# Head statistics aggregated on GpSimd instead of VectorE in a three-stage decoder kernel

## The reference

```
def _ln(x, w, b):
    mu = mean(x, axis=-1);  var = mean(square(x - mu), axis=-1)
    return (x - mu) * rsqrt(var + EPS) * w + b

q  = _ln(fp8_linear(ln_out, wq,  wq_s,  q_in_scale ).reshape(b, s, 8, 2, 128), qln_w,  qln_b)
k  = _ln(fp8_linear(ln_out, wk,  wk_s,  k_in_scale ).reshape(b, s, 8, 128),    kln_w,  kln_b)
qx = _ln(fp8_linear(ln_out, wqx, wqx_s, qx_in_scale).reshape(b, s, 8, 2, 128), qxln_w, qxln_b)
kx = _ln((cond @ w_kv_x.T)[k half], kxln_w, kxln_b)
core = softmax(q k^T / sqrt(128)) v;   xout = softmax(qx kx^T / sqrt(128)) vx
out  = fp8_linear(concat(core, xout), wproj)
```

## Time and profile before

| | |
|---|---|
| median of three runs | 1904.36 us (1903.78 to 1906.09) |
| profiled execution, its own time | 1905.79 us |
| its span | 1902.8 us |
| mean granted TensorE clock | 0.978 |
| TensorE busy (product, weight load) | 1789.1 us (94%), 1251.0 us (66%) |
| VectorE busy | 1506.1 us (79%), 4917 instructions |
| ScalarE busy | 1065.9 us (56%) |
| GpSimd busy | 269.1 us (14%), 417 instructions |

### The profile page before, as it was taken

How to read it: one execution, slowest core, us unless ns; L and a number is a source line. 1 busy time by engine, 2 the same in 40 slices (tenths; PEclk the granted TensorE clock), 3 DMA queues, 4 the chain that set the end, 5 groups by cost and what they waited for, 6 DMA issues and landing times.

```text
span 1902.8 us, 32280 instructions
## 1 busy us (share of the span) xinstructions
PE 1789.1 (94%) x11024; PEld 1251.0 (66%) x11024; DVE 1506.1 (79%) x4917; ACT 1065.9 (56%) x2478; POOL 269.1 (14%) x417
## 2 busy tenths in 40 slices
PE   7999999548999999999999999999999999879998
PEld 3444444236877778877777777887877777644554
DVE  0165747387888888898889888888878888888997
ACT  1121211115666766766766766677656666667776
POOL 0000000011111111112111111212111112101111
PEclk9999999868999999999999999999999999989999
DMA  6000000202110200101110111011010102210000
GB/s 222 22 1 23 1 1 1 75 4 67 36 36 15 64 25 25 58 23 35 34 47 25 45 36 36 12 58 34 14 30 17 47 16 76 69 65 12 23 25 32
DMA packets 40448, 70.77 MB, mean 37 GB/s; under 512 B 2912, under 2 KB 21856, under 8 KB 39264
## 3 DMA queue, kind: packets, MB, share of 16 engines
q1 hardware_dynamic: 40288, 68.73, 10.9%
HBM read 63.47 MB, written 4.19 MB: 36 GB/s over the span
## 4 chain that ended last, share of the span: by engine, by line
PE 71%; DVE 15%; issue 8%; POOL 2%; ACT 2%; DMA 1%; POOLq 0%; SPq 0%; DVEq 0%; ACTq 0%
PE bank L368 18%; PE bank L424 14%; PE bank L478 10%; PE bank L534 8%; PE bank L573 5%; PE bank L498 4%; PE bank L609 3%; PE bank L484 3%; PE bank L457 2%; PE bank L451 1%; DVE nq L1084 1%; DVE nmx L1190 1%; ACT yb L823 1%; PE bank L542 1%; POOL rsC L1369 1%
## 5 line engine op out<-in xcount | busy, mean ns | idle before, releaser
L835 ACT ACTIVATE pr<-bank,nmx 128x512 f32<-128x512 f32 x256 | 174.9, 692 | 144.5 <-DVE nmx L1190 144.2
L424 PE MATMUL bank<-wqs,XQ 128*128 128x256 f16 x2048 | 249.5, 276 | 4.4 <-DVE x L1114 4.4
L478 PE MATMUL bank<-prT,KV 128*128 128x256 f32 x1024 | 244.5, 382 | 0.1
L534 PE MATMUL bank<-kT,qT 128*128 128x512 f32 x512 | 242.5, 596 | 0.7 <-ACT kT L768 0.7
L424 PEld LDWEIGHTS bank<-wqs,XQ 128*128 128x128 bf16 x2048 | 199.6, 100 | 45.4 <-issue 15.7
L478 PEld LDWEIGHTS bank<-prT,KV 128*128 128x128 f32 x1024 | 191.2, 192 | 52.1 <-issue 22.8
L1335 POOL TENSOR_TENSOR rdev<-gvar,cst 128x7 f32<-128x7 f32 x128 | 193.2, 1509 | 10.0
L823 ACT ACTIVATE yb<-bank,rsT 128x128 bf16<-128x128 f32 x512 | 146.7, 373 | 62.2 <-PE bank L484 62.2
L1333 POOL TENSOR_TENSOR gvar<-mvB,geps 128x7 f32<-128x7 f32 x128 | 29.0, 227 | 1052.6 <-DVE mvB L1074 1045.2
L1190 DVE TENSOR_REDUCE nmx<-bank 128x1 f32<-128x512 f32 x256 | 166.4, 679 | 8.8 <-PE bank L534 5.7
L573 PE MATMUL bank<-identf,pr 128*128 128x128 f32 x1024 | 153.0, 278 | 19.3 <-DVE pr L1094 18.8
(11 more groups left out here) (162 smaller groups left out, 3245.8 us busy)
## 6 DMA issues: line engine op xcount, KB each, us to landing
wst<-in_wcat SPq DMA_DIRECT2D x24, 512.0 KB, 4.0
wpst<-in_wproj SPq DMA_DIRECT2D x8, 1024.0 KB, 5.2
wa<-in_wgu SPq DMA_DIRECT2D x16, 512.0 KB, 3.6
xT<-in_xT SPq DMA_DIRECT2D x4, 1024.0 KB, 5.2
x<-in_x SPq DMA_DIRECT2D x4, 1024.0 KB, 12.1
wkx<-in_wkvx SPq DMA_DIRECT2D x8, 512.0 KB, 5.0
wa<-in_wdn SPq DMA_DIRECT2D x8, 512.0 KB, 3.6
wst<-in_wgu SPq DMA_DIRECT2D x4, 1024.0 KB, 5.2
```

Of the source, the lines that this page charges most:

```text
L424: ins = mm(dst, XQ[:, b, c, k, j * P:(j + 1) * P], w, start=(k == 0 and m == 0), stop=(k == KT - 1 and m == 1))
L478: mm(OB[:, 0:2 * P], KV[:, n % 2, t, P:2 * P], prT[:, st % 2, t, :, :].rearrange("p h s -> p (h s)"), start=(t == 0), stop=(t == ST - 1))
L534: mm(SB_[h][:], qT[:, h, st * P:(st + 1) * P], kT[:, :], start=True, stop=True).then_inc(s["scores_made"], 1)
L835: act_f(pr[:, h, :], SB_[h][:], ACT.Exp, bias=nmx[:, st, h:h + 1], accum_out=su[:, st, h:h + 1]).then_inc(s["exp_done"], 1)
```

## The change

`head_stats` on VectorE keeps the bn_stats and loses the wait and the aggregations; the memset now gives the signal to GpSimd. `deviations` on GpSimd works from what bn_stats leaves for each slot, the means of two halves (columns 1 and 4) and their sums of squared differences (columns 2 and 5): the difference of the means squared times 32, plus the two sums, plus 128 times the epsilon, is 128 times the variance with its epsilon. The power -0.5 of that is the former `rdev` times 128^-0.5. The factor is made good in the tables: queries are scaled by the weight alone (`hln`), with the offset times 128^-0.5 in `hlq`; keys by the weight times 128^0.5 (`hlk`). The mean is half the sum of the half means (`mnB`).

```diff
-        hlq = sb(ctx, "hlq", [P, 4])
+        hlq = sb(ctx, "hlq", [P, 2])
+        hlk = sb(ctx, "hlk", [P, 2])
...
-        mvB = sb(ctx, "mvB", [P, 7, 2])
+        mnB = sb(ctx, "mnB", [P, 7])
+        smB = sb(ctx, "smB", [P, 4, 7])
...
-                                ACT.Identity, scale=hlq[:, 2 * c:2 * c + 1], bias=hlq[:, 2 * c + 1:2 * c + 2])
+                                ACT.Identity, scale=hln[:, 4 * c:4 * c + 1], bias=hlq[:, c:c + 1])
...
-                act_f(kT[:, :], MB[:, :], ACT.Identity, scale=hln[:, 2:3], bias=hln[:, 3:4]).then_inc(s["kt_out"], 1)
+                act_f(kT[:, :], MB[:, :], ACT.Identity, scale=hlk[:, 0:1], bias=hln[:, 3:4]).then_inc(s["kt_out"], 1)
...
-            own.do(v.tensor_scalar(hlq[:, 0:2], hln[:, 0:2], float(P) ** -0.5, None, ALU.mult))
-            own.do(v.tensor_scalar(hlq[:, 2:4], hln[:, 4:6], float(P) ** -0.5, None, ALU.mult))
+            for i in range(2):
+                own.do(v.tensor_scalar(hlq[:, i:i + 1], hln[:, 4 * i + 1:4 * i + 2], float(P) ** -0.5, None, ALU.mult))
+                own.do(v.tensor_scalar(hlk[:, i:i + 1], hln[:, 4 * i + 2:4 * i + 3], float(P) ** 0.5, None, ALU.mult))
...
-            v.tensor_scalar(geps[:], gain[:], EPS, None, ALU.mult).then_inc(s["hlq_ready"], 1)
+            v.tensor_scalar(geps[:], gain[:], EPS * P, None, ALU.mult).then_inc(s["hlq_ready"], 1)
...
-                own.do(v.memset(pad[:], 0.0))
-                own.sync()
-                for h in slots:
-                    ins = v.bn_aggr(mvB[:, h, :], bnB[:, h, :])
-                ins.then_inc(s["bn_ready"], 1)
+                v.memset(pad[:], 0.0).then_inc(s["bn_ready"], 1)
...
-            own.do(v.memset(mvB[:], 0.0))
+            own.do(v.memset(bnB[:], 0.0))
...
                 pool.wait_ge(s["bn_ready"], tile + 1)
-                own.do(g.tensor_tensor(gvar[:], mvB[:, :, 1], geps[:], ALU.add))
+                own.do(g.tensor_tensor(smB[:, 0, :], bnB[:, :, 1], bnB[:, :, 4], ALU.subtract))
+                own.do(g.tensor_tensor(smB[:, 1, :], bnB[:, :, 2], bnB[:, :, 5], ALU.add))
+                own.do(g.tensor_tensor(smB[:, 2, :], bnB[:, :, 1], bnB[:, :, 4], ALU.add))
+                own.sync()
+                own.do(g.tensor_tensor(smB[:, 0, :], smB[:, 0, :], smB[:, 0, :], ALU.mult))
+                own.do(g.tensor_tensor(smB[:, 1, :], smB[:, 1, :], geps[:], ALU.add))
+                own.do(g.tensor_tensor(mnB[:], smB[:, 2, :], cst[:, 3, 0:7], ALU.mult))
+                own.sync()
+                own.do(g.tensor_tensor(smB[:, 3, :], smB[:, 0, :], cst[:, 0, 0:7], ALU.mult))
+                own.sync()
+                own.do(g.tensor_tensor(gvar[:], smB[:, 3, :], smB[:, 1, :], ALU.add))
                 own.sync()
                 g.tensor_tensor(rdev[:], gvar[:], CPOW, ALU.pow).then_inc(s["stats_ready"], 1)
```

More of the change, by code:

```diff
@@ L767, in kt_out @@
                 act.wait_ge(s["kt_made"], n + 1)
-                act_f(kT[:, :], MB[:, :], ACT.Identity, scale=hln[:, 2:3], bias=hln[:, 3:4]).then_inc(s["kt_out"], 1)
+                act_f(kT[:, :], MB[:, :], ACT.Identity, scale=hlk[:, 0:1], bias=hln[:, 3:4]).then_inc(s["kt_out"], 1)
             def kxt_out(u):
                 act.wait_ge(s["kxt_made"], u + 1)
-                act_f(kxT[:, :], P1[:, 256:256 + P], ACT.Identity, scale=hln[:, 6:7], bias=hln[:, 7:8]).then_inc(s["kxt_out"], 1)
+                act_f(kxT[:, :], P1[:, 256:256 + P], ACT.Identity, scale=hlk[:, 1:2], bias=hln[:, 7:8]).then_inc(s["kxt_out"], 1)
             act.wait_ge(s["yA_made"], ST * NB)
@@ L1060, in head_stats @@
                     v.bn_stats(bnB[:, h, :], raw[:, h * P:(h + 1) * P])
-                slots = list(range(4))
                 for i, t in enumerate(KVPART[j]):
@@ L1065, in head_stats @@
                     v.bn_stats(bnB[:, 4 + i, :], KV[:, par, t, 0:P])
-                    slots.append(4 + i)
                 if j == 0 and n % 2 == 0:
@@ L1069, in head_stats @@
                     v.bn_stats(bnB[:, 6, :], kxr[:, :])
-                    slots.append(6)
-                own.do(v.memset(pad[:], 0.0))
-                own.sync()
-                for h in slots:
-                    ins = v.bn_aggr(mvB[:, h, :], bnB[:, h, :])
-                ins.then_inc(s["bn_ready"], 1)
+                v.memset(pad[:], 0.0).then_inc(s["bn_ready"], 1)
             def head_norm(n, j, par):
@@ L1079, in head_norm @@
                 if j == 0 and n % 2 == 0:
-                    v.tensor_scalar(kxn[:, :], kxr[:, :], mvB[:, 6, 0:1], rdev[:, 6:7], ALU.subtract, ALU.mult)
+                    v.tensor_scalar(kxn[:, :], kxr[:, :], mnB[:, 6:7], rdev[:, 6:7], ALU.subtract, ALU.mult)
                 for i, t in enumerate(KVPART[j]):
-                    v.tensor_scalar(kn[:, t, :], KV[:, par, t, 0:P], mvB[:, 4 + i, 0:1], rdev[:, 4 + i:5 + i], ALU.subtract, ALU.mult)
+                    v.tensor_scalar(kn[:, t, :], KV[:, par, t, 0:P], mnB[:, 4 + i:5 + i], rdev[:, 4 + i:5 + i], ALU.subtract, ALU.mult)
                 for h in range(4):
-                    ins = v.tensor_scalar(nq[:, j % 2, h * P:(h + 1) * P], raw[:, h * P:(h + 1) * P], mvB[:, h, 0:1], rdev[:, h:h + 1],
+                    ins = v.tensor_scalar(nq[:, j % 2, h * P:(h + 1) * P], raw[:, h * P:(h + 1) * P], mnB[:, h:h + 1], rdev[:, h:h + 1],
                                           ALU.subtract, ALU.mult)
```

## The result

| | before | after |
|---|---|---|
| median us (4 runs each) | 1904.07 (1903.66 to 1906.09) | 1923.55 (1922.55 to 1925.2) |
| profiled execution, own time / span | 1905.79 / 1902.8 | 1922.55 / 1920.6 |
| VectorE busy | 1506.1 | 1457.4 |
| GpSimd busy | 269.1 | 461.3 |

The ratio is 1.010, with a 95% interval of 1.0086 to 1.0114: 19.5 us slower, against a forecast of 11.2 and a range of 1906 to 1934.

A forecast was written before the change was run, and what follows sets the result against it. TensorE was taken to set the steady pace, alternating with VectorE from 1600 us on. Terms 6.2 + 3.6 + 1.4 + 0 = +11.2 us, put on the median 1904.36, gave 1915.6 us; range 1906 to 1934.

The forecast's parts named there:

- the new wait after tile 2: Steady part: VectorE newly waits half a microsecond to a whole one for `rdev`; TensorE projects meanwhile, cost taken as 0.
- the last pairs: Pairs 28 to 30: tile 0's loss, relief at tiles 1 to 3 and held-up GpSimd, between −1.6 and +3, taken as 0.
- few now: Sign at tile 0: TensorE's load waits for `pr` in few steady pairs before, nearly all after, 0.1 to 0.3 us.
- Steady, tile 0: Attention's steady part: later scaled rows stall TensorE 0.30 or 0.14 us, mean 0.22 in 28 pairs, +6.2 us.
- (b): GpSimd's sequence grows to eight small operations and the power: 1.68 us to the power instead of 0.28, adding 1.40.
- Tiles 1 to 3: Steady part: VectorE's other work or TensorE's projection covers GpSimd's longer sequence; 0 taken, up to 25 us if cover were gone.
- the thinnest place: Tile 3's rows, consumed in the next pair's st = 0: ready at 751.96, loaded at 752.26, usable slack 0.24 us.
- Start: 392 to 440 us: VectorE waits serially for `rdev` after each of four head tiles, TensorE waits too; +3.6 us.
- The sum across partitions: Near 1400 us: it keeps GpSimd away and VectorE waits 5.35 us; the whole added 1.40 counts, +1.4 us.
- The port: After tiles 1 and 3 VectorE's `round_terms` holds up GpSimd's small operations, tile 3 gives way: +17, 1932 us; chance 0.22.
- The hidden case: Steady tile 0: usable slack 0.3 us larger than read hides the stall; +3.4 us, 1908 us; chance 0.18.
- The relief case: Added GpSimd latency under 0.54 us brings `rdev` earlier, shrinking waits at end, start and steady part; 1894 us; chance 0.08.

The follow-up runs named there:

- b: The change with GpSimd's eight small operations replaced by one addition, no aggregation on either engine (statistics wrong); 1900.0 us, ratio 0.997 to the kernel before.
- c: The change for tiles 1 to 3 only, tile 0 keeping VectorE's aggregation and GpSimd's addition and power; 1912.5 us, 1.0034 of the kernel before.
- e: The change with GpSimd's sum across partitions moved from behind tile 1 to behind tile 3; 1916.8 us, 1.0059 of the kernel before.
- d: The change for tile 0 only, tiles 1 to 3 aggregating on VectorE as before; 1918.2 us, 1.0061 of the kernel before.
- k: The kernel before plus seven further GpSimd operations ahead of its addition at tiles 1 and 3 only; about 4 us above the expected 1911 us.
- a_latency: The kernel before plus the change's seven further GpSimd operations ahead of its addition, VectorE's aggregations kept; 1977.0 us, ratio 1.037.
- g: The kernel before with the sum across partitions behind tile 3 and GpSimd's addition and power on used slots only; 1898.7 us, 0.9962.
- i: g with the change's way of aggregating only for tiles of pairs 29 to 31, GpSimd operations interleaved; 1896.2 us, 0.9953 of the kernel before.

## Why the prediction was right, and what was mis-sized

**The mechanism held.** The direction, the place (tile 0, TensorE's load of scaled rows), VectorE's wait at tile 0 (about 2.1 us foretold, 2.16 measured) and at the start (about 3.3 foretold, 3.36 to 3.39 for the first three tiles), the new wait after tile 2 (0.80 us at 750.13), the worthlessness of VectorE's relief in the steady part (b: -0.01 to 0.03 a pair) and the last pairs (about 0 foretold, -0.48 us from pair 28 to 31) are as forecast. Three of the foretold signs did not come as written. TensorE's load waits for `pr` in more places than before (27 times against 17 between 500 and 1350 us, 14.9 us against 10.6), but at tile 0 the profile shows a wait only in pairs with six slots, and "few now" was wrong: the kernel before already waits in three pairs of four. The steady windows hold the same 1453 products. VectorE's busy time fell by 48.7 us and not by 58. Of the sum, four terms against the spans:

- **Steady, tile 0: +6.2 forecast, about 8.8 measured for all steady growth** (7.51 for 24 pairs, 0.96 for three more and 0.31 for the 28th, inside the step from pair 24 to 25). A pair grows by 0.31 us instead of 0.22. The mis-sized step is (b): small operations on seven elements stand 0.16 us apart, not the 0.14 of the one-element operations in the earlier trace rows, and the sequence adds 1.48 us instead of 1.40. With 0.08 us more, the loads at tile 0 would come 0.38 and 0.22 us later; they come 0.38 and 0.23 later. That this mean of 0.30 is nearly the growth of the pair is in part luck: the products behind the load come only 0.32 and 0.17 us later, a mean of 0.24, and the rest, 0.07 us in three pairs of four, is of the second place. A pair's growth is the difference of two nearly equal numbers, and a few hundredths in either are a third of it.
- **Tiles 1 to 3: 0 taken.** Right as a size (c grows by 0.03 a pair), but not as read: the earlier trace rows were taken for the thinnest place and are the pair of four that has room. In the other three there is no slack at all at st = 0.
- **Start: +3.6 forecast, 4.55 measured.** The four stretches from memset to `head_norm` grow by 0.96, 0.93, 1.00 and 1.06 us, 3.95 in all; against the forecast that is the same 0.08 four times. Of the rest, 0.25 us stood ahead of the first memset and 0.32 behind the last `head_norm`, both within what differs between executions of like programs.
- **The sum across partitions: +1.4 forecast, +4.2 measured** (4.49 less one steady step). This is the step that failed. The text let only the length of one sequence count, since "statistics were long ready". But GpSimd is a queue: tile 1's sequence stands ahead of the sum and is longer too, and tile 1's statistics themselves come later; and the wait ahead of the sum, in which nothing runs on GpSimd, was 2.3 us longer, for which no cause was found. e moves the term away with the sum, and d, with the old statistics at tiles 1 to 3, has only 0.38 there: it belongs to this place.

The forecast of 1915.6 was 8 us low; 2.8 of that are this term, 3.5 the steady part and the start, 0.3 the end and what lies behind. Another 1.7 are not in the spans at all: the profiled executions differ by 17.8 and the medians by 19.5. (The median of before, with the fourth run, lies 0.3 below the one that the forecast was put on.)

**The rivals.** The port stretches GpSimd, as its part of the trace foretold, but in tiles with room. Its price comes by way of VectorE's operations, and c and k put it at 0.03 us a pair, 1 us in all, where the rival had 17 (in the change 0.07 us in three pairs of four). Each held operation did wait for VectorE's to end, as the rival has it; but three of eight were held and not all, and each for the 0.06 to 0.23 us that were left of VectorE's. The hidden case would have needed the slack to be 0.3 us larger; the measured stall lies within 0.1 us of what the slack as read gives. The relief case had its decisive point at 0.54 us of added latency; b, with none added, gives 1900.0 and not 1894, since TensorE's waits for scaled rows in the steady part didn't shrink (11.2 us in 18 waits between 446 and 1380 us, and 11.1 in 18 before).

**What the text missed.** It called VectorE's relief worth nothing while TensorE has the pace. That is so from the kernel before (b). With GpSimd's longer sequence it isn't: a_latency has no relief and loses 72 us, the change 19.5. The relief paid for most of the latency that it brought along.

## What to carry to other kernels

Before moving work from a busy engine to an idle one, look for the place where the idle engine's latency is already waited for, and compare the added latency with the slack behind it; the busy share of either engine tells neither. A row of small operations on GpSimd cost its spacing here, 0.16 us each when independent and 0.28 when each waited for the last (730.13 to 730.29, 731.33 to 731.61), so interleave two chains and wait for single results instead of for all. An engine that works through its program in order hands a delay on to the rare, long job in it: put such a job into its longest free stretch. And a slack read in one period of a loop may not hold in the next: read it in every kind of period there is.

## What was not expected of the hardware

- The wait ahead of GpSimd's sum across partitions, in which nothing runs on it, varied with the program. It took 7.22 us in c, 7.44 in a_latency, 8.13 in k and 8.13 in the change, the four with the long sequence at tile 1 just ahead of it, and 5.72 to 6.39 in all others (5.87 in the kernel before). After it, 6.90 to 8.11 us passed before the next addition when work was ready. What decides it stays open.
- The power's time goes by elements a partition: undisturbed, 1.48 us for seven, 1.32 for six, 1.17 for five, 1.01 for four, while the small operations stay at 0.20 from four elements to seven.
- Holding up works in both directions: beside GpSimd's small operations VectorE's `cq`, otherwise 0.42 us, took 0.46 (738.80 in the change). Such hundredths reach TensorE where it waits for VectorE anyway.
- Two programs that are alike in a stretch can meet different granted clocks in it, as g and i do in the last products of stage C (1.00 and 0.57): 1.7 us, more than several of the effects measured here.
